# Splitting the state-space front of a hybrid kernel over two scans

## The chip, the cores and the metric

One core of a Trainium2 chip. The metric is the time of one execution in device microseconds. A core has a matrix engine (TensorE, PE in the profile; PEld is its weight load), a vector engine (VectorE, DVE), a scalar engine (ScalarE, ACT), GpSimd (POOL) and the queue that starts transfers (SyncE, SP). Each takes its instructions in the order written and waits for the others on semaphores. Matrix products land in PSUM, eight banks of 128 x 512 f32.

## The reference

Eight pictures of 128 channels x 1024 places pass through three stages, all in f32.

```python
x = x + conv_attention(group_norm(x))            # q, k, v of width 64, softmax over 1024 places
t = tokens(x)                                    # 1024 tokens x 128 channels
t = t + mamba(layer_norm(t))                     # mamba itself returns its input + a product
t = t + moe(layer_norm(t))                       # 8 experts, top 2, 128 -> 128 -> 128
# mamba(x): xn = rmsnorm(x); z, xBC, dt = split(xn @ W_in.T)
#   xBC = silu(causal_conv4(xBC)); xs, B, C = split(xBC); dt = softplus(dt + dt_bias)
#   state = state * exp(-dt*exp(A_log)) + (dt*xs) (x) B;  y = state . C + Dp*xs   (scan over tokens)
#   return x + rmsnorm(y * silu(z)) @ W_out.T
```

## The kernel before, in words

The work is ordered by hand. Each engine has a block of code, and in each the eight pictures go through three loops: `attended` (attention), `scanned(..., scan)` (the state-space stage) and `scanned(..., experts)`. Inside, a picture has eight slots (128 tokens each); parts with a number such as 3.5 are issued in that half slot, and parts with -0.25 or 6.75 just before the main work of a slot. No planner changes that order.

**Attention** (slots j). Scores go to banks 0-3 (L608, L613), VectorE takes the row maximum (L1455), ScalarE the exponential (L1104), PE turns the probabilities (`turn`, L641) through banks 4-5, ScalarE and VectorE copy them to `pt` (L1110, L1460), and `pv` (L654), `fold_parts` (L664) and `out_projection` (L673) use banks 6-7 (`O`). `projections` and `values` (L630, slot 5) of the next picture use `O` too. `residual` adds the result to `X[channel, place]` in slot 2.5. In slot 3 of the last picture VectorE prepares all weights of the next stage (`prepare_mamba`), and from there the front of picture 0 begins.

**The front** (`front` on VectorE, `pe_parts`, `act_parts`) turns a picture into what its scan reads. In order: copy `X` (`fetch`), turn it into tokens (`turn_in`, L755), statistics (L1560), a power on GpSimd (`norms`, L483), normed tokens `xt` (`normed`, L1166) and the residual `res` (`shortcut`, L1177) on ScalarE, `turn_normed` (L768), high and low parts (`high`, `low`), `steps` (L777) and three groups of projections (`group`, L730) each followed by a `tap` and three convolution steps on VectorE (`conv`, L1583), `softplus`, `cumulate` (L808), `exponents`, `factors`, the `gates`, `silus` with a table load at each end, `turn_x` (L801), `gather_x`, `turn_b`, `inner_products` (L829) and `inner` (L1639). SP writes and spreads the decay rows through DRAM (`decay_rows`), and `c_rep`. All products of the front share four banks, `lo_banks` (0-1) and `hi_banks` (2-3).

**The scan** of picture b (slots c): `decay(c + 1)` in banks 4-5 (L840), its exponential (`decays`, L1251), `mixed` on VectorE (L1654), `output_rows` (L867, L872, L879) and `y_t` (L1712). Beside it runs the whole front of picture b + 1: its first part in slot -0.25, its last in slot 7.5. In slot 0 PE also does `out_product` (L900) of picture b - 1 in `hi_banks`, and VectorE adds `res` to it (`output`, L1678). GpSimd makes `xdt`, and after slot 7 `decayed` (L514) and `weighted` (L524) of the next picture. In the last scan the front's place is taken by the start of the experts.

**Experts**: 16 halves per picture, bound by PE (L730 to L732, L983) and VectorE (L1832). The change doesn't touch them.

## Time and profile before

| | us |
|---|---|
| median of 3 runs | 1183.36 |
| lowest, highest | 1164.72, 1186.14 |
| the profiled execution | 1162.93 |
| its span, first to last instruction | 1161.1 |

The span is the profiled execution's own time less 1.8 us around it. The rows of the trace are from that execution alone. PEclk is the granted clock of TensorE: 1.00 is 2.4 GHz, 0.50 is 1.2 GHz, and a value between is a mean over a stretch that holds both.

### The profile page before, as it was taken

The numbers are of one execution on the slowest core, as the hardware profiler recorded it, in microseconds if no ns is written. First come the engines' busy times: TensorE is split into PE (matmuls) and PEld (weight loads), VectorE is DVE, ScalarE is ACT, GpSimd is POOL, SyncE is SP. The second block draws the span as 40 slices with busy tenths as digits, with TensorE's granted clock in tenths as the row PEclk, the third lists the DMA queues.
The fourth block names the chain that finished last, engine by engine and source line by source line (L and its number), as shares of the span: only waits on it lengthen the run. The fifth ranks groups of instructions, "written<-read, shape, count | busy, mean of one in ns | idle before, by whom it ended". The sixth has DMA issues, their size and how long they took to land.

```text
span 1161.1 us, 19636 instructions
## 1 busy us (share of the span) xinstructions
PE 939.0 (81%) x7630; PEld 730.8 (63%) x7630; DVE 708.1 (61%) x1846; ACT 547.2 (47%) x867; POOL 200.6 (17%) x186
## 2 busy tenths in 40 slices
PE   4689889988855678788687778698678999999998
PEld 2545565555533557576565656576567888888887
DVE  2865655565625365636556464646566888788875
ACT  1434444444433545454544535454532556555553
POOL 0000000000010505133150605142160111110100
PEclk9898899888975779888887979888888999999999
DMA  4300000000000203030301103030310000000000
GB/s 144 108 1 19 19 19 1 19 19 19 1 1 13 51 3 61 1 64 1 63 1 39 26 5 59 1 64 2 63 57 1 1 19 19 20 19 19 13 8 38
DMA packets 29613, 31.88 MB, mean 27 GB/s; under 512 B 4561, under 2 KB 24657, under 8 KB 29521
## 3 DMA queue, kind: packets, MB, share of 16 engines
q1 hardware_dynamic: 29520, 30.62, 10.8%
q8 instruction: 62, 1.02, 0.4%
q14 instruction: 31, 0.25, 0.1%
HBM read 17.24 MB, written 4.98 MB: 19 GB/s over the span
## 4 chain that ended last, share of the span: by engine, by line
PE 56%; DVE 26%; ACT 10%; issue 4%; POOL 3%; DMA 1%; SPq 1%; DVEq 0%; ACTq 0%; POOLq 0%
PE ps L983 6%; PE ps L654 5%; DVE cacc L1583 5%; PE ps L641 4%; DVE acc L1832 3%; PE ps L900 3%; POOL rs L483 3%; PE ps L630 3%; PE ps L879 2%; PE ps L872 2%; PE ps L840 2%; PE ps L867 2%; PE ps L730 2%; PE ps L888 2%; PE ps L731 2%
## 5 line engine op out<-in xcount | busy, mean ns | idle before, releaser
L1832 DVE SCALAR_TENSOR_TENSOR acc<-ps,comb,acc 128x128 f32<-128x128 f32 x512 | 141.2, 343 | 21.6 <-PE ps L983 20.9
L983 PEld LDWEIGHTS ps<-w_f,hid 128*128 128x128 f32 x1024 | 131.2, 191 | 16.5 <-ACT hid L1320 8.2
L983 PE MATMUL ps<-w_f,hid 128*128 128x128 f32 x1024 | 136.8, 277 | 4.8 <-ACT hid L1320 4.8
L1320 ACT ACTIVATE hid<-ps,b_f 128x512 f32<-128x512 f32 x128 | 86.2, 685 | 107.9 <-PE ps L732 107.6
L1251 ACT ACTIVATE dcy<-ps 128x1024 f32<-128x1024 f32 x64 | 65.7, 1027 | 141.8 <-PE ps L840 141.7
L1654 DVE SCALAR_TENSOR_TENSOR dcy<-dcy,g_sb 128x1024 f32<-128x1024 f32 x64 | 86.4, 1351 | 61.5 <-ACT dcy L1251 61.3
L1455 DVE TENSOR_REDUCE nmax<-ps 128x1 f32<-128x1024 f32 x64 | 78.1, 1220 | 40.0 <-PE ps L613 39.6
L1583 DVE SCALAR_TENSOR_TENSOR cacc<-ps,cw,cacc 128x1023 f32<-128x1023 f32 (+5 forms) x72 | 92.0, 1278 | 12.5 <-ACT cacc L1190 10.7
L1110 ACT ACTIVATE pt<-ps 128x512 f32<-128x512 f32 x64 | 38.1, 596 | 117.5 <-PE ps L641 117.2
L1460 DVE COPY pt<-ps 128x512 f32<-128x512 f32 x64 | 44.0, 688 | 76.7 <-PE ps L641 76.5
L641 PEld LDWEIGHTS ps<-id_f,probs 128*128 128x128 f32 x512 | 65.8, 156 | 34.6 <-issue 22.0
L1712 DVE TENSOR_TENSOR y_t<-ps,zs 128x256 f32<-128x256 f32 x64 | 26.7, 418 | 99.6 <-PE ps L879 99.6
L1104 ACT ACTIVATE probs<-ps,nmax 128x1024 f32<-128x1024 f32 x64 | 71.2, 1113 | 30.9 <-DVE nmax L1455 28.4
L641 PE MATMUL ps<-id_f,probs 128*128 128x128 f32 x512 | 77.3, 299 | 8.0 <-DVE pt L1460 7.9
L496 POOL TENSOR_TENSOR xdt<-xs,dts 128x256 f32<-128x256 f32 x64 | 42.5, 669 | 237.4 <-PE ps L879 237.4
L483 POOL TENSOR_TENSOR rs<-bve,neg_half 128x16 f32<-128x16 f32 x8 | 29.6, 3700 | 256.6 <-DVE bve L1569 256.6
L654 PE MATMUL ps<-pt,v_f 128*64 128x512 f32 x256 | 65.4, 617 | 3.2 <-DVE xl L1574 2.0
L867 PE MATMUL ps<-cacc,d_diag 128*128 128x128 f32 x256 | 52.7, 338 | 18.4 <-issue 16.0
L730 PE MATMUL ps<-uh,w_h 128*128 128x512 f32 x128 | 61.1, 477 | 0.0
L867 PEld LDWEIGHTS ps<-cacc,d_diag 128*128 128x128 f32 x256 | 42.2, 231 | 22.5 <-issue 18.8
L840 PE MATMUL ps<-rhs_c,lhs_c 128*128 128x512 f32 x128 | 55.8, 524 | 0.0
L608 PE MATMUL ps<-k_a,q_a 128*128 128x512 f32 x128 | 50.7, 480 | 5.7 <-ACT probs L1104 4.0
(214 smaller groups left out, 1935.2 us busy)
## 6 DMA issues: line engine op xcount, KB each, us to landing
c_dec<-exp_dram SPq DMA_DIRECT2D x32, 256.0 KB, 5.3
X<-in_x SPq DMA_DIRECT2D x8, 512.0 KB, 3.7
q_b<-q_a SPq DMA_DIRECT2D x16, 256.0 KB, 2.9
c_rep<-cacc SPq DMA_DIRECT2D x32, 128.0 KB, 2.6
out<-o_ch SPq DMA_DIRECT2D x8, 512.0 KB, 2.6
w_f<-in_w SPq DMA_DIRECT2D x2, 512.0 KB, 3.7
cst_f<-in_sel_rows SPq DMA_DIRECT2D x1, 512.0 KB, 4.0
cst_f<-in_head_rows SPq DMA_DIRECT2D x1, 512.0 KB, 5.6
```

Source lines behind the costliest of these rows:

```text
L641: last = nc.tensor.transpose(T[:, h, k * P:(k + 1) * P], probs[:, j % 2, (4 * h + k) * P:(4 * h + k + 1) * P], id_f[:])
L654: last = nc.tensor.matmul(O[e * DV:(e + 1) * DV, h, :], v_f[u][:, k, :], pt[u][:, k, h * BANK:(h + 1) * BANK], start=(quarter == 0), stop= ...
L730: nc.tensor.matmul(o, lhs[0], rhs[0], start=True, stop=False)
L840: done = nc.tensor.matmul(ps[:, 4 + h, :], lhs_c[u][:, c, :], rhs_c[u][:, 4 * h:4 * h + 4, :].rearrange("p h t -> p (h t)"), start=True, s ...
L867: nc.tensor.matmul(o[:, g, :], d_diag[:, g, :], cacc[u][:, g, t], start=(g == 0), stop=False, skip_group_check=True)
L983: last = nc.tensor.matmul(ps[:, Y_BANKS[n], t * P:(t + 1) * P], hid[n % 2][:, t * P:(t + 1) * P], w2_f[:, e, :], start=True, stop=True)
L1104: nc.scalar.activation(probs[:, j % 2, :].rearrange("p (a n) -> p a n", a=2), S[j % 2], ACT.Exp, bias=nmax[:, j:j + 1], accum_out=rsum[u][ ...
L1320: nc.scalar.activation(hid[n % 2][:], ps[:, 4 + n % 2, :], ACT.Gelu, bias=b1_f[:, n // 2:n // 2 + 1]).then_inc(e_hidden_ready, 1)
L1455: nc.vector.tensor_reduce(nmax[:, j:j + 1], S[j % 2], AX_XY, ALU.max, negate=True).then_inc(max_ready, 1)
L1583: ins = nc.vector.scalar_tensor_tensor(cacc[u][0:rows, g, k:N], banks[:, 0:N - k], cw[0:rows, g, DCONV - 1 - k:DCONV - k], cacc[u][0:rows, ...
L1654: nc.vector.scalar_tensor_tensor(mix[c % 2][:], dcy[c % 2][:], 1.0, g_sb[u][:, c:c + 1, :].to_broadcast([P, NH, P]), ALU.min, ALU.mult).th ...
L1832: done = nc.vector.scalar_tensor_tensor(acc[u][:, tt, :], ps[:, bank, t * P:(t + 1) * P], comb[u][:, tt, e:e + 1], acc[u][:, tt, :], ALU.m ...
```

## The change

- **Pictures and tokens apart.** `xc[:, b]` now holds the pictures as loaded for attention. `X` holds tokens (`X[token, chunk, channel]`), loaded from a second host-side arrangement `x_tok` by eight transfers that ScalarE's queue issues in picture 0 (two after slot 2, six after slot 6). GpSimd adds the output bias to `X` (`x_biased`). `out_projection` gives tokens: 16 products of 64 x 64 x 128 at positions (0, 0) and (64, 64) in place of 2 of 64 x 128 x 512. `residual` is one addition. `fetch`, `turn_in` and `res` are gone; `shortcut` rewrites `X` in place.
- **Statistics in attention.** `token_statistics` and `token_moments` of picture b - 1 are in VectorE's slots 5.5 and 7 of picture b, the power in GpSimd's `attend`. Those of pictures 6 and 7 follow after attention and in scan 0.
- **Attention order.** `values` from slot 5 to 5.5, `v_parts` from 5.5 to 6, `early_pv` from 6, 6.5, 7, 7.5 to 6.5, 7, 7, 7.5. One `pt` in place of two, with one more wait in slot 4.
- **Weight preparation** is cut into nine parts over pictures 2 to 6 (slots 0.5 and 6.5).
- **The front in two parts.** In scan b the late part (`cumulate` to `inner`) of picture b + 1 has slots -0.25 to 4, and the early part (`turn_normed` to the convolutions) of picture b + 2 slots 4 to 7.5. In scan 0 all are one slot later. `cacc` and `dts` have three buffers. `out_product(b - 1)` now waits for the last convolution of picture b + 1 (for the last two pictures: of the last `inner`). `gates` 1 wait for `output` of picture b - 1. GpSimd's `decayed` and `weighted` are in slots 3.5 and 4.5.
- **Between attention and scan 0**: the front of picture 0 begins in picture 7 of attention (`turn_normed` slot 3, group 0 slot 5, its convolution slots 5 to 7); the late part of picture 0 and the early part of picture 1 are written out by hand, partly among the last `pv`, `fold_parts` and `out_projection`; five convolution steps and one more of picture 1 stand in scan 0 (`second_front`).

The diff, cut to its core:

```diff
+        xc = asb("xc", [P, B, N])
+        cacc = [msb("cacc0", [P, 3, N]), cacc_1, cacc_2]
+        def slot_of(b, at):
+            return min(at + (b == 0), NT - 0.5)
...
# GpSimd
+            for b in range(B):
+                if b == 0:
+                    pool.wait_ge(tokens_loaded[0], 16 * 2)
+                elif b == 2:
+                    pool.wait_ge(tokens_loaded[1], 16 * (B - 2))
+                xb = X[:, b, :].rearrange("p (t c) -> p t c", c=P)
+                nc.gpsimd.tensor_tensor(xb, xb, b_o[:]...to_broadcast([P, NT, P]), ALU.add).then_inc(x_biased, 1)
+            decayed_at, weighted_at, norms_at = 3.5, 4.5, 2.5
...
# TensorE
-                for e in range(2):
-                    r = slice(64 * e, 64 * e + 64)
-                    last = nc.tensor.matmul(O[:, 1 - e, :], w_o[r, :], o_n[r].rearrange("p j v -> p (j v)"), ...)
+                for j in range(NT):
+                    for e in range(2):
+                        r = slice(64 * e, 64 * e + 64)
+                        last = nc.tensor.matmul(O[r, j // 4, j % 4 * P:(j % 4 + 1) * P], o_n[r, j, :], w_o[r, :],
+                                                start=True, stop=True, tile_position=(64 * e, 64 * e))
-            projections_at, values_at = 3, 5
-            early_pv = [6, 6.5, 7, 7.5]
+            projections_at, values_at = 3, 5.5
+            early_pv = [6.5, 7, 7, 7.5]
...
             def out_product(b):
                 pe.wait_ge(m_gated_ready, NT * b + NT)
-                if not isinstance(b, int) or b < B - 1:
-                    pe.wait_ge(m_inner_ready, b + 2)
+                if b + 2 < B:
+                    pe.wait_ge(m_conv_ready, 3 * (b + 2) + 3)
+                else:
+                    pe.wait_ge(m_inner_ready, B)
...
-            pe_parts = [(turn_normed, (), 1.5), (group, (0, 0), 3), (group, (0, 1), 3), (steps, (), 3),
-                        (group, (1, 0), 3.5), (group, (1, 1), 3.5), (group, (2, 0), 4.5),
-                        (group, (2, 1), 4.5), (cumulate, (), 5), (gates, (0, 0), 6), (gates, (0, 1), 6),
-                        (gates, (1, 0), 6), (gates, (1, 1), 6), (turn_x, (0,), 6), (turn_x, (1,), 6),
-                        (turn_b, (), 6.75), (inner_products, (), 7.5)]
+            pe_parts = [(cumulate, (), 1, -0.25), (gates, (0, 0), 1, 0.5), (gates, (0, 1), 1, 0.5),
+                        (gates, (1, 0), 1, 1.5), (gates, (1, 1), 1, 1.5), (turn_x, (0,), 1, 2.5),
+                        (turn_x, (1,), 1, 2.5), (turn_b, (), 1, 3), (inner_products, (), 1, 3.5),
+                        (turn_normed, (), 2, 4), (steps, (), 2, 5), (group, (0, 0), 2, 5), (group, (0, 1), 2, 5),
+                        (group, (1, 0), 2, 5.5), (group, (1, 1), 2, 5.5), (group, (2, 0), 2, 6.75),
+                        (group, (2, 1), 2, 6.75)]
...
# ScalarE
+                    if first and j in (2, 6):
+                        for k in range(2) if j == 2 else range(2, B):
+                            nc.scalar.dma_start(X[:, k, :], x_tok[k]).then_inc(tokens_loaded[j // 4], 16)
-            act_parts = [(fetch, (), 0), (normed, (), 1.5), (high, (), 2), (shortcut, (), 2.5),
-                         (steps, (), 3), (tap, (0,), 3), (softplus, (), 4.75), (tap, (1,), 4.75),
-                         (factors, (), 5), (tap, (2,), 5), (silus, (), 6), (gather_x, (), 7),
-                         (gather_b, (), 7.5)]
+            act_parts = [(factors, (), 1, 0), (shortcut, (), 1, 0.5), (silus, (), 1, 1.5), (gather_x, (), 1, 2.75),
+                         (gather_b, (), 1, 3.5), (normed, (), 2, 3.5), (high, (), 2, 4.5), (steps, (), 2, 5.5),
+                         (tap, (0,), 2, 5.5), (softplus, (), 2, 6), (tap, (1,), 2, 6), (tap, (2,), 2, 7)]
...
# VectorE
+            preparations = {(2, 6.5): (scale_weights, ()), (3, 0.5): (scale_outputs, ()), (3, 6.5): (high_weights, ()),
+                            (4, 0.5): (decay_operands, (0, 0)), (4, 6.5): (decay_operands, (0, 1)),
+                            (5, 0.5): (decay_operands, (1, 0)), (5, 6.5): (decay_operands, (1, 1)),
+                            (6, 0.5): (low_weights, ()), (6, 6.5): (small_weights, ())}
-                return [(statistics, (), -0.25), (low, (), 2), (conv, (0, 1), 3.5), (conv, (0, 2), 3.5),
-                        (conv, (0, 3), 3.5), (steps, (), 3.5), (conv, (1, 1), 4), (conv, (1, 2), 4),
-                        (conv, (1, 3), 4), (softplus, (0,), 4.5), (softplus, (1,), 4.5),
-                        (exponents, (), 4.5), (conv, (2, 1), 5), (conv, (2, 2), 5), (conv, (2, 3), 5),
-                        (ends, (), 7), (inner, (), 7.5)]
+            dve_parts = [("exponents", (), 1, -0.25), ("ends", (), 1, 1), ("inner", (), 1, 4), ("low", (), 2, 4.5),
+                         ("steps", (), 2, 5.5), ("conv", (0, 1), 2, 5.5), ("conv", (0, 2), 2, 5.75),
+                         ("conv", (0, 3), 2, 6), ("softplus", (0,), 2, 6), ("softplus", (1,), 2, 6),
+                         ("conv", (1, 1), 2, 6.5), ("conv", (1, 2), 2, 6.75), ("conv", (1, 3), 2, 7),
+                         ("conv", (2, 1), 2, 7.5), ("conv", (2, 2), 2, 7.5), ("conv", (2, 3), 2, 7.5)]
+            statistics_at, moments_at = 5.5, 7
```

## Rows read from the trace of the kernel before

**Rows 1.** The page: the chain that ended last, share of the span by engine.

```profile
PE 56%; DVE 26%; ACT 10%; issue 4%; POOL 3%; DMA 1%; SPq 1%; DVEq 0%; ACTq 0%; POOLq 0%
```

**Rows 2.** Windows: stretch, us; busy PE, PEld, DVE, ACT, POOL; PEclk, DMA share, GB/s.

```profile
159.10:196.80 37.70, 33.98 (x169) 21.71 (x169) 21.34 (x26) 17.05 (x28) 0.00 (x0) 0.91 0.07 15
...
309.00:334.20 25.20, 11.32 (x61) 9.22 (x62) 15.78 (x45) 12.64 (x29) 3.28 (x3) 0.70 0.00 0
334.20:391.80 57.60, 37.66 (x162) 25.17 (x161) 20.13 (x32) 21.33 (x25) 6.98 (x6) 0.68 0.16 32
...
585.70:650.70 65.00, 50.85 (x574) 40.96 (x574) 36.87 (x74) 32.44 (x52) 19.44 (x18) 0.84 0.14 29
...
846.00:893.30 47.30, 37.27 (x500) 30.94 (x499) 30.45 (x94) 14.06 (x25) 16.20 (x15) 0.78 0.10 35
```

**Rows 3.** Windows of short stretches in an attention picture and in scan 3.

```profile
203.30:206.70 3.40, 1.23 (x5) 0.71 (x5) 3.31 (x4) 2.97 (x5) 0.00 (x0) 0.96 0.64 139
206.70:213.40 6.70, 6.70 (x28) 6.14 (x28) 2.46 (x3) 1.80 (x3) 0.00 (x0) 0.51 0.04 8
...
618.30:622.90 4.60, 0.00 (x0) 0.00 (x0) 4.49 (x6) 0.98 (x1) 0.00 (x0) 0.99 0.00 0
623.00:632.90 9.90, 8.38 (x52) 6.35 (x53) 7.36 (x17) 3.22 (x6) 0.62 (x1) 0.50 0.08 23
```

**Rows 4.** Timeline of PE, attention picture 4: start, us, instruction [idle before].

```profile
206.67 3.67 PE L630 MATMUL ps<-w_v,xn 128*128 128x64 f32 x16 [2.06 <-DVE k_a L1440]
...
232.60 1.13 PE L673 MATMUL ps<-o_n,w_o 64*128 64x512 f32 x4
```

**Rows 5.** Timeline of PE, last picture of attention, from slot 5 on.

```profile
320.03 2.30 PE L641 MATMUL ps<-id_f,probs 128*128 128x128 f32 x8 [4.96 <-DVE pt L1460]
...
332.27 1.94 PE L768 MATMUL ps<-id_f,xt 128*128 128x128 f32 x8 [6.54 <-ACT res L1177]
```

**Rows 6.** Timeline of DVE, the end of the first front.

```profile
389.55 1.22 DVE L1639 TENSOR_TENSOR g_sb<-ps,tri_f 128x1024 f32<-128x1024 f32 x1 [14.16 <-PE ps L829]
391.83 1.58 DVE L1654 SCALAR_TENSOR_TENSOR dcy<-dcy,g_sb 128x1024 f32<-128x1024 f32 x1 [1.06 <-ACT dcy L1251]
```

**Rows 7.** Timeline of DVE: the first `mixed` of scans 3, 4 and 7.

```profile
583.43 2.80 DVE L1654 SCALAR_TENSOR_TENSOR dcy<-dcy,g_sb 128x1024 f32<-128x1024 f32 x1 [0.57 <-ACT dcy L1251]
...
648.38 1.58 DVE L1654 SCALAR_TENSOR_TENSOR dcy<-dcy,g_sb 128x1024 f32<-128x1024 f32 x1 [0.57 <-ACT dcy L1251]
...
843.32 1.60 DVE L1654 SCALAR_TENSOR_TENSOR dcy<-dcy,g_sb 128x1024 f32<-128x1024 f32 x1 [0.57 <-ACT dcy L1251]
```

**Rows 8.** Timeline of PE in scan 3.

```profile
624.52 0.69 PE L808 MATMUL ps<-dec_a,tri_f 128*128 128x64 f32 x2 [6.30 <-DVE dec_a L1613]
...
647.96 3.81 PE L900 MATMUL ps<-w_out,y_t 128*128 128x128 f32 x32
```

**Rows 9.** Timeline of ACT in scan 3: the two table loads around `silus`.

```profile
632.52 1.28 ACT L1203 ACT_TABLE_LOAD   x1
...
638.94 1.28 ACT L1209 ACT_TABLE_LOAD   x1
```

**Rows 10.** Timeline of SP, picture 0: one transfer's issue.

```profile
43.54 0.47 SPq L400 DMA_DIRECT2D q_b<-q_a  x1
```

**Rows 11.** Groups: line, engine, operation, tiles, shapes xcount | busy us, mean ns | idle before.

```profile
L1583 DVE SCALAR_TENSOR_TENSOR cacc<-ps,cw,cacc 128x1023 f32<-128x1023 f32 (+5 forms) x72 | 92.0, 1278 | 12.5 <-ACT cacc L1190 10.7
L1654 DVE SCALAR_TENSOR_TENSOR dcy<-dcy,g_sb 128x1024 f32<-128x1024 f32 x64 | 86.4, 1351 | 61.5 <-ACT dcy L1251 61.3
...
L1251 ACT ACTIVATE dcy<-ps 128x1024 f32<-128x1024 f32 x64 | 65.7, 1027 | 141.8 <-PE ps L840 141.7
...
L1166 ACT ACTIVATE xt<-ps,rnb,rs 128x128 f32<-128x128 f32 x64 | 23.2, 467 | 22.1 <-POOL rnb L487 22.1
...
L1712 DVE TENSOR_TENSOR y_t<-ps,zs 128x256 f32<-128x256 f32 x64 | 26.7, 418 | 99.6 <-PE ps L879 99.6
...
L524 POOL TENSOR_TENSOR xw<-xs,wend 128x1024 f32<-128x1024 f32 (+1 forms) x16 | 33.7, 2122 | 0.0
```

504 lines of the change are left out of this document (301 added, 203 removed).

## The prediction

> **What bounds the kernel now.** Read the page's chain first. TensorE holds 56% of it and VectorE 26%, with ScalarE, GpSimd and transfers in between [rows 1]: no single engine sets the time, a chain through all of them does. Then cut the span into its stages. An attention picture takes 37.7 us with PE busy for 34.0, so it is nearly full. From 309 to 391.8 us comes the passage to the scans, 82.8 us at clocks of 0.70 and 0.68 with PE busy for 11.3 + 37.7. A scan takes 65.0 us, in which PE is busy for 50.9 at a mean clock of 0.84, VectorE for 36.9 and ScalarE for 32.4 [rows 2]. The first `mixed` of scan 0 is at 391.8 and that of scan 7 at 843.3 [rows 6, 7], so the mean period is (843.3 - 391.8) / 7 = 64.5 us, and 317.8 us follow (scan 7 and the experts).
>
> PE's own work in a scan, at the full clock, is about 50.9 x 0.84 = 43 us. The other 22 us are waits and the low clock. The waits are the front's: PE stands for 6.30 us before `cumulate`, for VectorE's convolutions and softplus [rows 8]; it is idle from 618.3 to 622.9, and after it the clock is 0.50 for 9.9 us [rows 3], which costs some 4 to 5 us more. All of the front of picture b + 1 must pass within scan b, for it begins in its slot 0 and `inner` ends it after slot 7. That is the bound the change is aimed at.
>
> **Part 1, attention, seven pictures up to 309 us.** PE waits 2.06 us for `k_low` before `values`, and `values` with what follows runs 6.7 us at a clock of 0.51 [rows 3, 4]. One turn of probabilities (about 1.0 us; the 2.30 of one at the low clock halves to 1.15 [rows 5]) now goes first. It fills about half of the wait: -1.0 us. PE was busy for 1.23 of the 3.4 us before the clock fell [rows 3] and will be for some 2.2. If the clock then stays up, half of 6.7 us, 3.4, is saved; if not, nothing. I take the middle, -1.7. `out_projection` grows from 4 instructions in 1.13 us [rows 4] to 32 narrower ones. One of 128 columns costs 3.81 / 32 = 0.12 us when alone [rows 8]; by that it is 3.8 us, and 1.9 if the two positions run beside each other. The 64-row pair of before, two products of 512 columns in 1.13 us where eight passes at that price (4 blocks of 128 columns x 4) are 1.9, shows that pairs do overlap: +0.8, bound +2.7. It stands between `divide` and `residual`, which `projections` wait for, so it counts. VectorE gets the statistics, 2.7 us, and a seventh of the weight preparation, 1 us; its 21.3 busy of 37.7 [rows 2] leave room, so 0, bound +3.7 if each delays a maximum. Sum -1.9 per picture, -13 for seven; between -4.4 and +5.4 each. Eight transfers issued by ScalarE at 0.47 us [rows 10] are 3.8 us of its queue in picture 0, the exponentials of that picture and the next behind them: +2. GpSimd's eight additions run while it has nothing else. The second copy of `x` adds 4 MB before about 80 us; the first `q_b` of picture 2 may wait a little (0 taken, bound +4). The changed wait on the single `pt` is for a product that PE has already passed: 0. Attention: -11.
>
> **Part 2, the passage, 82.8 us.** In the last picture two stops go: 4.96 us, where PE waits behind the weight preparation on VectorE, and 6.54, where it waits for statistics, power, `normed` and `shortcut` [rows 5]. In exchange the last picture carries `normed` twice (8 x 0.47 each [rows 11]), `high`, one group and three convolutions (1.28 each [rows 11]). Slots run at some 2.6 us there, so the last turn ends about 309 + 13 + 5 = 327 instead of 336. After it (clock times of the trace of before): the last `pv` with group 1 and 2, `fold_parts` until 343; `exponents` 347, since they stand on VectorE behind two convolutions of group 2 that follow `divide`; gates 350; the block of `silus` from first to last table load is 7.7 us [rows 9], silus done at 355; `c_rep` through SP 5 us, 360; `inner_products` and `inner` (which ended at 390.8 [rows 6]) 363. VectorE then does the early part of picture 1 before it starts scan 0: `low` 1.2, `steps`, tap, three convolutions 3.8, softplus 2, in all 12 us, 375; `shortcut` and `decays(0)` on ScalarE end at about 376. Of that PE does some 33 us at the full clock, and this stretch ran at 0.68 [rows 2]; most of PE's low-clock work lies beside the others, +4. First `mixed` 380 against 391.8: -12. Bounds -22 (all products beside VectorE) and 0 (each at the low clock).
>
> **Part 3, scans 1 to 5.** Walk the cycle, with t = 0 where VectorE ends the last convolution of group 2 (now in slot 7.5, behind `y_t` of slot 7). `out_product` waits for it (3.8 us [rows 8]); then `cumulate`, `decay(1)`, `output_rows(0)`, increments, gates 0, `decay(2)`: 10.7. Its exponential 1.0, `mixed` 1.2, `output` 2.2: 15.2. Gates 1 wait for that `output`; they and the rest of the 7.7 us block of `silus` end at 22. `decays(3)` stands behind the block on ScalarE, so `mixed(3)` and `y_t` are late there. ScalarE then has `decays`, `gather_x`, `gather_b` and `normed` (3.8 by the rows' mean, overlapped 2.9) in a row [rows 11]; `high` ends at 32.5 and `low` at 35.1. `steps`, group 0 and `output_rows(5)` on PE: 41. From there VectorE never stops: nine convolutions 11.5, `mixed(7)` 1.2, two `y_t` 0.8 [rows 11], steps, softplus and one more `y_t` 3.4: 58. So the cycle is closed again, only turned round: the early part's end on VectorE now holds up `out_product`, as `inner` did. What has gone from it is the statistics, the power and `normed` ahead of `turn_normed`, `turn_in`, and part of the 6.3 us wait. What is late next is VectorE's run of 17 us at the end, with PE idle for about 7 of the last 12 us. A stretch like it (618.3 to 622.9) was followed by a clock of 0.50 [rows 3]; half of the first 6 us, 3, and 1.5 behind the waits for `output` and the narrow `steps` give 62.5, and GpSimd's moved work 0.5: 63 us, against 64.5. Bounds: 42 (PE's 43 less `turn_in`, nothing waiting) and 77 (42 at a clock of 0.68, 62, and 15 of waits). I take 63, near the walk. Five scans: 315.
>
> **Part 4, scans 0, 6 and 7.** Scan 0 has no `out_product`, but five to six more convolutions (7 us) and all parts one slot later: 62. Scan 6 has only a late part: `inner` at about 33, then slots 5 to 7 at 3 us, no run of convolutions: 44. This is the surest gain, 20 us. Scan 7 and the experts are as before, 317.8.
>
> One rule of the Trainium skill speaks against the change. GpSimd's `weighted` (2.1 us an instruction [rows 11]) stood beside one `mixed` per scan, the first: that took 2.80, 1.58 and 1.60 us [rows 7] where the mean of all is 1.35 [rows 11]. The page "SBUF — State Buffer", section "SBUF: two separate sides", says that a VectorE instruction with two SBUF inputs and a GpSimd instruction exclude each other for the whole instruction. By that rule the trace agrees (`mixed` reads two SBUF tiles), and `decayed` and `weighted`, now in slots 3.5 and 4.5, meet `mixed(5)` and `mixed(6)`.
>
> **Sum.** 391.8 - 11 - 12 = 368.8; + 62 + 315 + 44 + 317.8 = 1107.6; + 1.8 around the span = 1109.4, against 1162.93 of the profiled execution. The median of the three runs shown is 1183.36, 20 above it, and the lowest is 1164.72. I put 6 of those 20 on top: 1115.
>
> **Rivals.**
> - *The split works in full.* The chain no longer closes on itself, and a scan takes what its engines need with little waiting, 52 us (PE 42 and 10 of waits). Six scans less 10 each: 1055. For it: no engine is busy for more than 51 of 65 us. Against: the walk, where `out_product` waits for the convolutions. 0.13.
> - *The chain is only turned round, and the clock gives nothing.* Attention as before, scans 0 to 5 at 65: 391.8 - 12 + 390 + 44 + 317.8 + 1.8 = 1133. For: all parts still share four banks in one order. 0.23.
> - *GpSimd blocks the middle of the scan.* `mixed(5)` and `mixed(6)` lie on the path to `low`; each loses up to 1.6 us (2.80 less 1.2 [rows 7]), less the 0.5 taken and 0.4 no longer lost at the start. Two us more in six scans: 1121 to 1127. 0.17.
> - *Slower: the low clock fills the scan.* If VectorE's run of 17 us leaves PE at 1.2 GHz for as large a share as in the passage (0.68 [rows 2]), a scan takes 77 us: 6 x 14 = 84 more, 1199. It decides above 72 us a scan. Against: three quarters of the scan keep PE as dense as before. 0.05.
>
> **Chances.** The forecast 0.42, the rivals 0.13, 0.23, 0.17 and 0.05. The range 1062 to 1158 takes in the first three and half of what lies between the last and the forecast. Two per cent, about what a measurement of this kernel tells from no change, is 23 us: faster 0.85 (the second rival lies near the edge), within 0.10, slower 0.05.
>
> **What would show it.** Right: scan period of scans 1 to 5 at 61 to 65, scan 6 near 44, first `mixed` near 369; PE's longest wait before `out_product`, released by a convolution (`cacc`), and none before `cumulate`; VectorE without gaps from `y_t` of slot 5 to slot 7.5; no wait of `turn_normed` for `xt`; the clock up where `values` run in attention. Wrong: a period under 56 or above 67, attention pictures above 38 us, the clock near 0.7 in scans, or a wait for `x_updated` or `tokens_loaded` in attention.

## Result, and the profile after

| | median, us | lowest to highest | runs |
|---|---|---|---|
| kernel before | 1174.04 | 1162.19 to 1186.14 | 4 |
| changed kernel | 1118.02 | 1115.9 to 1120.57 | 4 |

The ratio is 0.959, with a 95% interval of 0.953 to 0.965: faster. Two runs of the kernel before (1183.36 and 1186.14 us) fell into a slower state that some executions show whatever the kernel; the ratio leaves them out, and against the other two (1162.19 and 1164.72) the gain is 45 us, where the two medians of the table are 56 apart. The forecast was 1115. The profiled execution took 1116.23 us (span 1114.4), where the sum of the prediction was 1109.4; that execution is the one to compare term by term. The kernel before is the noisier of the two (24 us between its extremes, against 4.7 here), so the stages below are compared in the two profiled executions: 1162.93 and 1116.23, 46.7 us apart.

The page of the changed kernel, its busy times and its chain, where [rows 1] had PE 56%, DVE 26% and ACT 10%:

```profile
PE 928.4 (83%) x7790; PEld 737.3 (66%) x7790; DVE 712.2 (64%) x1838; ACT 542.2 (49%) x859; POOL 236.8 (21%) x194
...
PE 53%; DVE 28%; ACT 8%; issue 6%; POOL 2%; DMA 1%; SPq 1%; DVEq 0%; ACTq 0%; POOLq 0%
...
L1773 DVE SCALAR_TENSOR_TENSOR dcy<-dcy,g_sb 128x1024 f32<-128x1024 f32 x64 | 95.4, 1491 | 117.9 <-ACT dcy L1310 117.5
```

The kind of bound has not changed: still a chain through all engines. It has only become shorter. Its stages, by the starts of the residual and of the first `mixed` of each scan on VectorE (us):

| stage | before | predicted | after | after, less predicted |
|---|---|---|---|---|
| residual of picture 6 | 309.04 | 298.0 | 293.51 | -4.5 |
| passage, to the first `mixed` | 82.8 | 70.8 | 71.8 | +1.0 |
| scan 0 | 62.4 | 62 | 63.6 | +1.6 |
| scans 1 to 5 together | 324.0 | 315 | 318.6 | +3.6 |
| scan 6 | 65.2 | 44 | 47.7 | +3.7 |
| from scan 7 to the end of the span | 317.8 | 317.8 | 319.2 | +1.4 |

The last column adds up to 6.8 us, which is the difference between 1116.2 and 1109.4. The windows of the changed kernel that answer to [rows 2]: one attention picture, the passage, scan 0, scan 3 and scan 6 (columns as in [rows 2]).

```profile
153.46:188.46 35.00, 31.58 (x197) 20.42 (x197) 24.60 (x46) 16.98 (x28) 3.28 (x3) 1.00 0.07 16
293.50:365.30 71.80, 50.16 (x276) 37.87 (x276) 36.99 (x74) 37.63 (x59) 12.76 (x11) 0.83 0.13 26
365.30:428.90 63.60, 48.95 (x532) 39.04 (x532) 42.00 (x69) 31.64 (x51) 18.42 (x16) 0.77 0.14 30
554.60:619.20 64.60, 51.39 (x566) 42.79 (x565) 35.20 (x54) 31.65 (x51) 19.07 (x15) 0.82 0.14 29
748.62:796.31 47.69, 43.16 (x533) 35.95 (x532) 20.24 (x33) 23.80 (x36) 20.30 (x15) 0.81 0.20 40
```

The passage went from clocks of 0.70 and 0.68 to 0.83. Scan 3 has the busy times and nearly the clock of before (50.9 busy at 0.84 then): the split front made the full scans barely shorter, by 5.4 us in all five. The gain lies in three other places: attention (15.5 us), the passage (11.0), and scan 6, which no longer carries an early part (17.5). Scan 0 and the last stage take back 1.3 and 1.4. Attention and a part of the passage are tested by runs below. That scan 6 is shorter for want of an early part is read from its rows; no run isolates it.

**Attention.** TensorE around `values` of picture 4 after the change, to be laid beside [rows 4]:

```profile
198.21 2.00 PE L660 MATMUL ps<-w_v,xn 128*128 128x64 f32 x16 [0.34 <-DVE k_a L1524]
...
203.56 1.08 PE L684 MATMUL ps<-pt,v_f 128*64 128x512 f32 x4 [1.51 <-DVE v_f L1533]
...
221.43 1.96 PE L705 MATMUL ps<-w_o,o_n 64*64 64x128 f32 x32
```

The wait before `values` fell from 2.06 to 0.34, and the same 16 products take 2.00 us instead of 3.67: the clock stays at 1.00, the upper of its two levels. `out_projection` is at the predicted 1.9. A wait that I had not named, 1.51 us for `v_f`, is new, and so is one of 0.66 for `pt`; the wait for `X` before the projections fell from 1.02 to 0.29. PE is therefore idle almost as long as before, 3.4 us of a picture instead of 3.7 (35.00 less 31.58, 37.70 less 33.98 [rows 2]). What became shorter is the time of the products, by 2.4 us, or 3.2 without the 0.8 that `out_projection` adds.

**Scan 3.** VectorE and TensorE from one turn to the next; t = 0 of the prediction's walk is 553.4 here.

```profile
553.69 6.19 PE L947 MATMUL ps<-w_out,y_t 128*128 128x128 f32 x32 [2.83 <-DVE cacc L1682]
...
570.04 0.80 PE L763 MATMUL ps<-xh,w_zh 128*128 128x512 f32 x1 [2.94 <-DVE X L1798]
...
592.87 0.38 PE L810 MATMUL ps<-w_dt,xh 128*128 128x16 f32 x1 [3.04 <-DVE xl L1673]
...
607.89 0.50 PE L763 MATMUL ps<-xh,w_xh 128*128 128x512 f32 x1 [2.25 <-DVE cacc L1682]
```

```profile
567.83 2.15 DVE L1798 SCALAR_TENSOR_TENSOR X<-ps,srs,X 128x128 f32<-128x128 f32 x8
...
579.24 1.22 DVE L1773 SCALAR_TENSOR_TENSOR dcy<-dcy,g_sb 128x1024 f32<-128x1024 f32 x1 [8.78 <-ACT dcy L1310]
...
582.30 2.31 DVE L1773 SCALAR_TENSOR_TENSOR dcy<-dcy,g_sb 128x1024 f32<-128x1024 f32 x1 [1.50 <-ACT dcy L1310]
...
587.32 2.77 DVE L1773 SCALAR_TENSOR_TENSOR dcy<-dcy,g_sb 128x1024 f32<-128x1024 f32 x1 [2.37 <-ACT dcy L1310]
...
591.60 1.22 DVE L1673 TENSOR_TENSOR xl<-ps,xh 128x1024 fp32r<-128x1024 f32 x1
...
601.61 0.42 DVE L1836 TENSOR_TENSOR y_t<-ps,zs 128x256 f32<-128x256 f32 x1 [7.66 <-PE ps L924]
...
618.09 1.21 DVE L1773 SCALAR_TENSOR_TENSOR dcy<-dcy,g_sb 128x1024 f32<-128x1024 f32 x1
```

GpSimd beside the two slow `mixed`:

```profile
581.44 5.12 POOL L536 TENSOR_TENSOR c_dec<-c_dec,c_rep 128x896 f32<-128x896 f32 x2 [2.25 <-DMA c_rep<-cacc]
...
587.10 4.33 POOL L546 TENSOR_TENSOR xw<-xs,wend 128x1024 f32<-128x1024 f32 x2
```

`cumulate` waits for nothing any more, and `out_product` waits 2.83 us for the last convolution. It then takes 6.19 us, where [rows 8] had 3.81: it runs at the lower clock level. PE has two more waits of the same size, 2.94 us for `output` and 3.04 for `low`. From `y_t` of slot 5 at 601.61 on, VectorE has no gap until the next turn at 619.3.

### The profile page after: what moved, and what is told of

It reads as the page before. It is cut to its first block, busy times and chain, and to the rows that moved or that the text cites. A ratio compares the mean times of both kernels' runs of the same rounds, so it can differ in the third digit from the quotient of the medians.

```text
span 1114.4 us, 20011 instructions
## 1 busy us (share of the span) xinstructions
PE 928.4 (83%) x7790; PEld 737.3 (66%) x7790; DVE 712.2 (64%) x1838; ACT 542.2 (49%) x859; POOL 236.8 (21%) x194
## 3 DMA queue, kind: packets, MB, share of 16 engines
q1 hardware_dynamic: 29520, 30.68, 11.3%
## 4 chain that ended last, share of the span: by engine, by line
PE 53%; DVE 28%; ACT 8%; issue 6%; POOL 2%; DMA 1%; SPq 1%; DVEq 0%; ACTq 0%; POOLq 0%
PE ps L1028 6%; DVE cacc L1682 6%; PE ps L684 5%; PE ps L947 4%; PE ps L763 3%; DVE acc L1959 3%; PE ps L765 3%; PE ps L764 3%; PE ps L671 3%; DVE nmax L1539 2%; PE ps L638 2%; ACT X L1234 2%; ACT un L1354 2%; PE ps L883 2%; PE ps L643 2%
## 5 line engine op out<-in xcount | busy, mean ns | idle before, releaser
L1773 DVE SCALAR_TENSOR_TENSOR dcy<-dcy,g_sb 128x1024 f32<-128x1024 f32 x64 | 95.4, 1491 | 117.9 <-ACT dcy L1310 117.5
L1028 PEld LDWEIGHTS ps<-w_f,hid 128*128 128x128 f32 x1024 | 131.2, 191 | 16.5 <-ACT hid L1373 8.2
L518 POOL TENSOR_TENSOR xdt<-xs,dts 128x256 f32<-128x256 f32 x64 | 58.3, 913 | 211.6 <-PE ps L924 211.6
L671 PEld LDWEIGHTS ps<-id_f,probs 128*128 128x128 f32 x512 | 60.0, 144 | 32.5 <-issue 22.9
L671 PE MATMUL ps<-id_f,probs 128*128 128x128 f32 x512 | 70.0, 280 | 8.7 <-ACT pt L1169 6.7
L684 PE MATMUL ps<-pt,v_f 128*64 128x512 f32 x256 | 63.6, 611 | 9.3 <-DVE v_f L1533 9.3
L947 PE MATMUL ps<-w_out,y_t 128*128 128x128 f32 x256 | 44.9, 357 | 20.4 <-DVE cacc L1682 20.4
L505 POOL TENSOR_TENSOR rs<-bve,neg_half 128x16 f32<-128x16 f32 x8 | 23.2, 2903 | 180.2 <-DVE bve L1587 180.2
L763 PE MATMUL ps<-uh,w_h 128*128 128x512 f32 x128 | 61.1, 477 | 0.0
L947 PEld LDWEIGHTS ps<-w_out,y_t 128*128 128x128 f32 x256 | 43.6, 270 | 20.7 <-issue 20.7
L883 PE MATMUL ps<-rhs_c,lhs_c 128*128 128x512 f32 x128 | 50.5, 480 | 7.0 <-ACT dcy L1310 7.0
L933 PEld LDWEIGHTS ps<-ones_f,sqt 128*128 128x128 f32 x256 | 43.4, 226 | 19.0 <-DVE y_t L1836 13.6
```

The costliest lines, as they stand in the source:

```text
L671: last = nc.tensor.transpose(T[:, h, k * P:(k + 1) * P], probs[:, j % 2, (4 * h + k) * P:(4 * h + k + 1) * P], id_f[:])
L684: last = nc.tensor.matmul(O[e * DV:(e + 1) * DV, h, :], v_f[u][:, k, :], pt[:, k, h * BANK:(h + 1) * BANK], start=(quarter == 0), stop=(qu ...
L763: nc.tensor.matmul(o, lhs[0], rhs[0], start=True, stop=False)
L883: done = nc.tensor.matmul(ps[:, 4 + h, :], lhs_c[u][:, c, :], rhs_c[u][:, 4 * h:4 * h + 4, :].rearrange("p h t -> p (h t)"), start=True, s ...
L947: last = nc.tensor.matmul(cols(hi_banks, c, P), y_t[:, g, c * P:(c + 1) * P], w_out[:, g, :], start=(g == 0), stop=(g == 1))
L1028: last = nc.tensor.matmul(ps[:, Y_BANKS[n], t * P:(t + 1) * P], hid[n % 2][:, t * P:(t + 1) * P], w2_f[:, e, :], start=True, stop=True)
```

## Experiments

Twelve kernels were run, in three groups, each on one chip and beside the kernel before on that chip. The median of the kernel before was 1166.66, 1171.87 and 1161.51 us in the three; the changed kernel, run once more in the third, gave 1118.61 against the first 1118.02. The first two groups had no run of the changed kernel on their chip. Differences "to the changed kernel" below go by these two numbers; differences under 3 us are read from the stages alone. "Scans 1 to 5" are always the five periods of the profiled execution.

### The order in attention, taken back and done alone

Taken back in the changed kernel:

```diff
-projections_at, values_at = 3, 5.5
+projections_at, values_at = 3, 5
-early_pv = [6.5, 7, 7, 7.5]
+early_pv = [6, 6.5, 7, 7.5]
-... statistics_at, moments_at = 1.5, 2.5, 5.5, 7
+... statistics_at, moments_at = 1.5, 2.5, 6, 7
-... v_at = 1.5, 4, 4.5, 6
+... v_at = 1.5, 4, 4.5, 5.5
```

> The changed kernel with the old slots in attention (values 5, v_parts 5.5, first pv 6; the statistics go to slot 6 so that they do not stand before v_parts). Theory: the 2.65 us per picture come from the order alone, by a shorter wait before values and by the clock that stays up behind it. Then a picture takes 37.5 to 38.5 us again, the clock is near 0.50 for about 6.8 us in each, and the kernel takes 18 to 24 us more, near 1140. Rival: the shorter picture comes from the single addition of the residual and the other rearrangements, and the order does nothing: within 4 us of the changed kernel.

Measured: 1138.95 us (1132.01 to 1141.37), ratio to before 0.977 (0.969 to 0.984), 21 us above the changed kernel. The last four pictures take 37.7 to 37.8 us again (the six periods are 38.3, 36.2, 37.8, 37.8, 37.7 and 37.7) and the residual of picture 6 starts at 310.72. In this run the row and the clock of before are back, here `values` and the window behind them:

```profile
207.27 3.68 PE L660 MATMUL ps<-w_v,xn 128*128 128x64 f32 x16 [2.08 <-DVE k_a L1524]
```

```profile
207.20:213.90 6.70, 6.63 (x28) 6.18 (x28) 2.45 (x4) 1.47 (x2) 0.00 (x0) 0.50 0.05 10
```

In the picture that takes 36.2 us `values` waited just as long, but ran at the upper level, and the clock fell only behind them (0.95 over that picture, 0.91 over those of 37.8):

```profile
133.32 2.00 PE L660 MATMUL ps<-w_v,xn 128*128 128x64 f32 x16 [2.08 <-DVE k_a L1524]
```

In the pictures of 37.8 us PE is idle for 3.0 us (37.80 less 34.82), less than the 3.4 of the changed kernel's 35.0. So the whole gain of the order lies in the clock and none in the sum of the waits.

Done alone, in the kernel before:

```diff
-projections_at, values_at = 3, 5
+projections_at, values_at = 3, 5.5
-early_pv = [6, 6.5, 7, 7.5]
+early_pv = [6.5, 7, 7, 7.5]
-... v_at = 1.5, 4, 4.5, 5.5
+... v_at = 1.5, 4, 4.5, 6
```

> The kernel before with nothing changed but the slots of values (5.5), v_parts (6) and the pv (6.5, 7, 7, 7.5). Theory (order and clock): 34 to 35 us a picture (its out_projection is 0.8 us shorter than the changed kernel's), 18 to 25 us less than before in all. Rival (the rest of the change shortens the picture): within 5 us of before.

Measured: 1149.78 us (1142.83 to 1165.72), ratio 0.983 (0.976 to 0.990), 17 us under the kernel before on that chip. `values` fall to 2.00 us with a wait of 0.35:

```profile
195.81 2.00 PE L630 MATMUL ps<-w_v,xn 128*128 128x64 f32 x16 [0.35 <-DVE k_a L1440]
```

Pictures take 34.6 us, 3.1 less, and the first `mixed` comes at 373.33 instead of 391.83. So this order (a turn of probabilities ahead of `values`, `v_parts` and the first `pv` half a slot later) is worth all that attention gained and a little more; its three moves were not tried one by one. The changed kernel's pictures are 0.4 us longer (35.0); its `out_projection` costs 0.8 there. In the profiled execution 11.2 of the 18.5 us reach the end: scan 6 took 69.4 us there, against 65.2 before.

### The weight preparation put back in one place

```diff
-preparations = {(2, 6.5): (scale_weights, ()), (3, 0.5): (scale_outputs, ()), ...}
+preparations = {}
...
+                    if last and j == 3:
+                        prepare_all()
```

> The changed kernel with all nine parts of the weight preparation in slot 3 of the last picture, as before. Theory: PE waits for VectorE there as it did (4.96 us), so 4 to 6 us more, all of it before the first mixed. Rival: the earlier pictures get shorter by as much without the parts: within 1 us. A third: other waits of the last picture hide it, 0 to 2 us more.

Measured: 1123.66 us (1121.59 to 1128.7), ratio 0.964 (0.959 to 0.968): 5 to 6 us more than the changed kernel, as the first account has it. The last picture takes 43.0 us against 34.8 and the first `mixed` comes at 374.48, 9.2 later. The wait of 4.96 us for `pt` of [rows 5] is back at 4.00:

```profile
304.96 0.66 PE L671 MATMUL ps<-id_f,probs 128*128 128x128 f32 x4 [4.00 <-DVE pt L1551]
```

In the span the two profiles differ by 12.5 us, 9.2 of them here; the medians say 5 to 6.

### GpSimd's two steps put back at the end of the scan (a miss)

```diff
-                if slot == slot_of(b, decayed_at) and not last:
-                    decayed(b + 1, 1 - u)
-                if slot == slot_of(b, weighted_at) and not last:
-                    weighted(b + 1, 1 - u)
...
+                        decayed(b + 1, 1 - u)
                         operand(b + 1, 1 - u, 0)
+                        weighted(b + 1, 1 - u)
```

> The changed kernel with GpSimd's decayed and weighted behind slot 7 again. Theory: mixed(4) and mixed(5), which took 2.31 and 2.77 us in scan 3, fall to 1.22, and they lie on the way to low: 2 to 2.6 us less in each of scans 1 to 5, 8 to 15 us in all; the blocked mixed(0) at the start costs nothing, for PE waits for the convolution. Rival: they have slack, or the lost time is taken back at the start, where xdt(0) is late: within 4 us.

Measured: 1130.9 us (1128.64 to 1133.32), ratio 0.970 (0.965 to 0.975): 12 to 13 us slower than the changed kernel, where I had expected a gain. Scans 1 to 5 took 67.3, 65.2, 70.4, 65.9 and 66.8 us. The trace shows both halves. `mixed(4)` and `mixed(5)` are at 1.23 us again. But GpSimd's instructions now stand beside VectorE's unbroken run at the end of the scan, where nothing is idle:

```profile
530.55 1.23 DVE L1771 SCALAR_TENSOR_TENSOR dcy<-dcy,g_sb 128x1024 f32<-128x1024 f32 x1 [1.51 <-ACT dcy L1308]
...
550.96 2.67 DVE L1771 SCALAR_TENSOR_TENSOR dcy<-dcy,g_sb 128x1024 f32<-128x1024 f32 x1
...
554.74 1.28 DVE L1702 TENSOR_SCALAR dtw<-dte 128x64 f32<-128x64 f32 x1
```

```profile
548.41 4.13 POOL L536 TENSOR_TENSOR c_dec<-c_dec,c_rep 128x896 f32<-128x896 f32 x2
...
554.06 3.35 POOL L546 TENSOR_TENSOR xw<-xs,wend 128x1024 f32<-128x1024 f32 x2
```

```profile
554.88 0.80 PE L761 MATMUL ps<-xh,w_xh 128*128 128x512 f32 x1 [4.10 <-DVE cacc L1680]
```

Even the small softplus step at 554.74, 0.18 us in the changed kernel, takes 1.28, and PE waits 4.10 us before group 2 instead of 2.25. From `mixed(7)` to the first `mixed` of the next scan VectorE takes 12.7 us in each of the five full scans of the changed kernel, and 15.7 to 16.0 in this run: 3 us a scan, about what the scans lost. The cost that I had priced at 0.5 us a scan is real, about 2.6 us on the two `mixed`; but the place the change gave these steps is better than the old one.

### What sets the full scans: output first, filler, cumulate first

Three single edits of the changed kernel. The first lets VectorE do `output(b - 1)` before `mixed(2)`, which stands ahead of it in a wait:

```diff
+                    if c == 1 and not first:
+                        output(b - 1, 1 - u)
                     if c < NT - 1:
                         mixed(b, u, c + 1)
-                    if c == 1 and not first:
-                        output(b - 1, 1 - u)
```

> The changed kernel with output(b - 1) ahead of mixed(2) on VectorE in slot 1. Theory: gates 1 wait for it (2.94 us in scan 3, on the path to silus), and it waits for nothing that is late; about 1.7 us of idle VectorE before mixed(2) and its 1.2 us leave the path, 2 to 3 us less in each of scans 1 to 5, and more where the clock no longer falls behind that wait: 10 to 25 us less in all. Rival: mixed(2) is then late and output_rows(2) takes its place as the last wait: within 3 us.

Measured: 1104.45 us (1098.52 to 1107.89), ratio 0.944 (0.936 to 0.951), 14 us under the changed kernel. Scans 1 to 5: 59.2, 61.5, 61.4, 61.5, 61.4. The wait for `X` before the gates is gone, and `silus` passes both gates in one go:

```profile
569.35 1.94 ACT L1260 ACTIVATE zs<-ps 128x1024 f32<-128x1024 f32 x2
```

The second fills two waits of PE at the turn with products whose result nobody reads, 8 before the last `y_t` and 11 before the last convolution:

```diff
+                            if b < B - 1:
+                                pe.wait_ge(m_gated_ready, NT * b - 1)
+                                filler(6, 8)
                             pe.wait_ge(m_gated_ready, NT * b)
                             sum_of_squares(b - 1, NT - 2)
                             sum_of_squares(b - 1, NT - 1)
+                            if b < B - 1:
+                                pe.wait_ge(m_conv_ready, 3 * (b + 1) + 2)
+                                filler(1, 11)
                             out_product(b - 1)
```

> The changed kernel with products nobody reads on PE in its two waits at the end of a scan: 8 before the wait for y_t(7), 11 between the sums of squares and out_product. They only keep PE busy. Theory: out_product runs at a clock of 0.50 in scans 1 to 5 (6.2 to 6.6 us instead of 3.8) because of the waits; with them filled it takes 3.8 us and each scan is 2 to 3 us shorter, 8 to 14 in all. Rival: the low clock there has another cause or is moved elsewhere: within 4 us, or longer by the filler itself.

Measured: 1107.92 us (1105.17 to 1119.61), ratio 0.950 (0.938 to 0.962), 10 us under the changed kernel. `out_product` takes 3.74 to 3.81 us in the five full scans:

```profile
551.08 2.70 PE L941 MATMUL ps<-ones_f,id_f 128*128 128x128 f32 x22
...
554.05 3.81 PE L952 MATMUL ps<-w_out,y_t 128*128 128x128 f32 x32 [0.27 <-DVE cacc L1693]
```

PE does more work and the kernel is faster: what `out_product` lost in the changed kernel, 2.4 us in scan 3, is the clock that falls in the waits at the turn, and nothing in `out_product` itself. Scans 1 to 5 together are 308.2 us against 318.6.

Part of the gain is given back further on. Here is the stretch from `mixed(4)` to `mixed(5)` of scan 3, in which PE does `inner_products`, first in the changed kernel, then with the filler:

```profile
582.30:587.32 5.02, 5.02 (x65) 4.31 (x63) 2.65 (x3) 4.67 (x12) 5.02 (x4) 1.00 0.02 5
```

```profile
578.98:588.24 9.26, 9.26 (x63) 7.67 (x63) 2.76 (x3) 4.65 (x12) 8.16 (x5) 0.50 0.01 3
```

The low clock has gone from the turn and turned up here, in scans 2 to 4, which is what the second account had allowed for. It costs 4.2 us there; by `mixed(3)` the filler had put scan 3 3.7 us ahead. The version with `output` first has the same 9.26 us at 0.50 in scans 2 to 4.

The third puts work with a far shorter wait at the turn: `cumulate` ahead of the sums of squares, and `decay(1)` ahead of `out_product`:

```diff
+                            pieces(b, -0.25)
                             sum_of_squares(b - 1, NT - 2)
                             sum_of_squares(b - 1, NT - 1)
+                            decay(b, u, 1)
                             out_product(b - 1)
-                    pieces(b, c - 0.25)
-                    if c + 1 < NT:
-                        decay(b, u, c + 1)
+                    if c > 0 or first:
+                        pieces(b, c - 0.25)
+                        if c + 1 < NT:
+                            decay(b, u, c + 1)
```

> The changed kernel with cumulate before the sums of squares and decay(1) before out_product on PE. Both need nothing of the last convolution. Theory: the head of the cycle is out_product, then cumulate, exponents, decay(1), mixed(1); with them out of it VectorE makes exponents and mixed(1) while out_product runs, and only output_rows(0), increments and gates 0 stay behind it: 1.5 to 2.5 us less per scan, 7 to 13 in all. Rival: the cycle is closed by engines' work and not by this order: within 3 us.

Measured: 1109.41 us (1106.82 to 1117.59), ratio 0.952 (0.943 to 0.960), 9 us under. Scans 1 to 5: 66.4, 62.0, 61.0, 61.9, 61.1. `out_product` waits 1.14 us instead of 2.83 and is still 6.28 us long, so what is gained at the turn is of the chain, not of the clock. The two edits of order together:

> Both of the last but one and the first of this set together (cumulate and decay(1) ahead of out_product; output ahead of mixed(2)). Theory: two different waits of one chain, so the gains add: 17 to 35 us less than the changed kernel. Rival: after one of them another branch ends last: no more than the better of the two.

Measured: 1091.24 us (1090.25 to 1095.16), ratio 0.935 (0.929 to 0.940), 27 us under the changed kernel, where the two alone gave 14 and 9. Scans 1 to 5: 62.4, 58.7, 61.0, 57.8, 58.1. The clock at the turn is still the lower one, by the window of its `out_product`:

```profile
553.60:560.00 6.40, 6.40 (x36) 6.40 (x36) 2.92 (x7) 3.50 (x10) 2.31 (x2) 0.60 0.10 28
```

### The last convolutions shortened (a miss in size)

Is VectorE's run at the end the bound of the scan? For pictures 2 to 7 the second and third step of group 2 work on 8 columns only; the rest of these two steps is left out of the computation.

```diff
+                    end = k + 8 if b >= 2 and g == 2 and k >= 2 else N
-... cacc[b % 3][0:rows, g, k:N], banks[:, 0:N - k], ...
+... cacc[b % 3][0:rows, g, k:end], banks[:, 0:end - k], ...
```

> The changed kernel with the second and third convolution step of group 2 done for 8 columns only, for pictures 2 to 7; the rest of those two steps is left out. It takes 2 x 1.1 us from VectorE's run before out_product in scans 0 to 5. Theory: that run closes the cycle, so each of those scans is 2.2 us or more shorter (more where PE then waits less and its clock stays up): 13 to 25 us in all. Rival: another chain ends beside it (products or ScalarE), and it has slack: within 4 us.

Measured: 1113.22 us (1110.26 to 1116.11), ratio 0.959 (0.954 to 0.963). That is 5.4 us under the changed kernel run beside it, between what the two accounts expected, so it decides for neither. The wait before `out_product` fell to 0.73 us, and `out_product` to 5.44:

```profile
553.55 5.44 PE L947 MATMUL ps<-w_out,y_t 128*128 128x128 f32 x32 [0.73 <-DVE cacc L1683]
```

Scans 1 to 5 took 62.7, 61.7, 61.2, 65.1 and 61.2, in all 311.9 against 319.1 in the changed kernel beside it; and scan 6 took 52.7 against 45.3, which gives the whole of it back in this execution. Scan 6 has no convolutions, and the edit takes nothing from it; what grew is the clock's part. From its `mixed(4)` on it ran like this:

```profile
767.60:776.90 9.30, 9.30 (x63) 7.82 (x63) 2.75 (x3) 1.65 (x5) 8.19 (x5) 0.50 0.00 1
776.90:793.59 16.69, 16.69 (x173) 12.30 (x173) 6.51 (x9) 4.67 (x8) 1.85 (x3) 0.62 0.00 1
```

In the changed kernel beside it the first of these stretches took 5.00 us at 1.00, and the second this:

```profile
786.40:797.74 11.34, 10.81 (x170) 8.15 (x163) 8.06 (x8) 4.80 (x8) 6.79 (x5) 1.00 0.01 3
```

PE was busy without a gap at the lower level; what let the clock fall there, this run does not show. What it does show is that VectorE's run at the end counts, for less than its length.

### Filler in the best version, and `silus` in another order

The changed kernel stood beside these two and the one with short convolutions, unedited:

> The changed kernel, unchanged, on the chip of the next three: 1114 to 1122 us. It is the measure for them.

Measured: 1118.61 us (1115.64 to 1121.02, 6 runs), ratio 0.964 (0.961 to 0.967): the first result again.

The filler of 8 products ahead of the last `y_t`, added to the version with both edits of order:

> The kernel with cumulate, decay(1) and output ahead, and with 8 unread products on PE before its wait for y_t(7). Theory: out_product there still runs at 0.50 (6.24 us); if PE's wait of 2.15 us is what lets the clock fall, it takes 3.8 us and scans 1 to 5 are 1 to 2.5 us shorter, 5 to 12 in all, near 1082. Rival: the remaining waits of the run (1.6 and 1.1 us) are enough to let it fall: within 4 us of 1091.

Measured: 1093.05 us (1087.97 to 1105.4), ratio 0.945 (0.939 to 0.951); without its highest run the median is 1091.47: no gain. `out_product` stays wholly or partly at the lower clock in four of the five full scans (5.0 to 6.6 us). In three of them a wait of 1.3 us is left in front of it that this filler doesn't cover:

```profile
547.77 6.57 PE L952 MATMUL ps<-w_out,y_t 128*128 128x128 f32 x32 [1.32 <-DVE cacc L1693]
```

That wait alone does not decide it: in scan 4 it is as long, 1.31 us, and `out_product` takes 3.81.

Last, in that kernel the block of `silus` takes its three convolution results before the two gates, because `c_rep` (through SP's queue) and with it `inner_products` wait for the third of them:

```diff
-                for g in range(2):
-                    act.wait_ge(m_z_product, 3 * b + 2 + g)
-                    nc.scalar.activation(two(zs[u][:, g, :]), ...)
...
+                for g in range(2):
+                    act.wait_ge(m_z_product, 3 * b + 2 + g)
+                    nc.scalar.activation(two(zs[u][:, g, :]), ...)
```

> As the one before, and ScalarE's silus takes the three convolution results before the two gates. Theory: in the changed kernel the block waited 3.7 us for gates 1, but with output ahead that wait is gone, so the order inside the block of 7.4 us changes little; c_rep starts 3 us earlier, but inner_products wait for gather_x too: within 3 us of the one before. Rival: turn_x(0) and c_rep are on the path: 1 to 3 us less per scan, 6 to 18 in all.

Measured: 1077.03 us (1074.47 to 1079.27), ratio 0.928 (0.924 to 0.933): 16 us under the one before by the medians, 14 without that kernel's highest run and 12.6 in the profiled executions; 41 to 42 under the changed kernel, and the fastest of all. Scans 1 to 5: 55.7, 58.2, 58.4, 54.1, 58.2. The transfer is issued 15.5 us after the `mean_square` that marks the scan (559.86 less 544.40), against 17.4 in the kernel without this edit (566.10 less 548.68). SP's issue of it here, then VectorE's mark:

```profile
559.86 2.45 SPq L460 DMA_DIRECT2D c_rep<-cacc  x4
```

```profile
544.40 0.15 DVE L1800 TENSOR_SCALAR sve<-ps 128x8 f32<-128x8 f32 x1
```

The same two in the kernel without the edit:

```profile
566.10 2.44 SPq L460 DMA_DIRECT2D c_rep<-cacc  x4
```

```profile
548.68 0.15 DVE L1800 TENSOR_SCALAR sve<-ps 128x8 f32<-128x8 f32 x1
```

The transfer goes 1.8 to 2.0 us earlier in each of the five scans. Yet this is not what made them shorter: without the edit they took 62.4, 57.8, 58.8, 60.7 and 58.2 us, so scans 2, 3 and 5 stayed within 0.4 us, and scans 1 and 4 lost 6.7 us each, 13.3 in all. From `mixed(4)` to `mixed(6)` of scan 1, without the edit and with it:

```profile
449.93:465.78 15.85, 15.27 (x111) 11.89 (x110) 6.68 (x6) 7.00 (x15) 8.78 (x6) 0.53 0.00 1
```

```profile
451.96:461.30 9.34, 7.47 (x100) 5.76 (x100) 6.06 (x7) 7.17 (x15) 8.61 (x6) 1.00 0.01 2
```

Scan 4 shows nearly the same numbers (15.86 us at 0.53, 9.35 at 1.00), and in scan 3 the stretch takes 10.44 us at 0.87 without the edit and 10.25 at 0.87 with it. So the gain is 6.5 us of clock in the middle of each of two scans. The rival's result came, and its reason, that `c_rep` is on the path, is not borne out by the three scans in which `c_rep` came earlier and nothing followed. Why the clock stays up with this order is not shown. The wait of PE before `decay(4)` is 2.18 us without the edit in scan 1, and split into 0.80 and 1.18 with it, which may be the reason. The edit was not tried in the changed kernel alone.

## Why the prediction was right

The time (1118.0, forecast 1115), the sign and every stage to within 5 us came as predicted, in the main for the reasons given. In attention and in the passage part of the closeness is luck: errors in two terms went opposite ways. Point by point, by its steps:

- **Part 1, attention, -11: the sign and the clock right, two terms mis-sized.** Predicted were -1.0 for the wait, -1.7 for the clock, taken as the middle between 0 and 3.4, and +0.8 for `out_projection`. The wait before `values` lost 1.7 us (2.06 to 0.34) and that before the projections 0.7, but 1.5 for `v_f` and 0.7 for `pt` came in: the waits together give only -0.3. They moved and did not go. From `values` to the first `pv` it was 6.85 us (206.67 to 213.52) and is 5.35 (198.21 to 203.56), of which 1.51 are the new wait for `v_f`: the work itself lost 3.0, near the upper end. With +0.8 that is -0.3 - 3.0 + 0.8 = -2.5 of the 2.7 by which a picture is shorter (37.7 to 35.0). So 0.7 too much for the wait stood against 1.3 too little for the clock. The sum has two slips that changed nothing: the bound of -4.4 leaves out the +0.8, and the "eight passes" that make 1.9 are sixteen (4 x 4). The +2 for ScalarE's eight issues and the bound of +4 for the second copy of `x` came to nothing: the seventh residual is 15.5 us earlier, and the first of all, 83.3 against 83.6, is not late. The two runs with the order of attention show that this edit carries the whole term: 17 us when taken back, 20 when done alone (309.04 less 289.08), at the residual of picture 6.
- **Part 2, the passage, -12: right, -11.0.** The two stops went as said: in the last picture PE's longest wait is 2.10 us, and `turn_normed` waits for nothing. The stations fit too. Counted from the residual of picture 6, `c_rep` was to be there after 51 us and PE starts `inner_products` after 50.9; from the end of `inner` to the first `mixed` 17 us were taken and 15.9 came (349.4 to 365.3). That the 51 us came out is partly luck: `silus` was done after 42.4 us, where 46 were taken, and `c_rep` then took 8.2 us from issue to PE (336.11 to 344.28) in place of 5. It is in the chain with 6.27 us, of PE's wait for it 4.45. The weight preparation, when put back, is worth 9.2 us up to the first `mixed`, 5 to 6 in the median.
- **Part 3, scans 1 to 5, 63 us: right, 63.7 in the mean (62.7, 61.9, 64.6, 64.2, 65.2).** The statement that the chain is "only turned round" held: `out_product` now waits for the last convolution, 2.83 us, and `cumulate` for nothing. It is not PE's longest wait, as I had said it would be; those for `output` and `low`, 2.94 and 3.04 us, are as long. In scan 3, counted from 553.4, `output` ended at 16.6 (walk: 15.2), `low` at 39.4 (35.1), `y_t` of slot 5 came at 48.2 (41), and VectorE's run took 16.5 us (17). The 7 us by which the walk is exceeded at slot 5 stand against the 5 that I had put on top of it as one sum. The 2.4 us in `out_product` are the clock term, and the filler shows its cause. The 0.5 for GpSimd was too small: the two `mixed` lost 1.1 and 1.5 us, and they are `mixed(4)` and `mixed(5)`, where the prediction had (5) and (6). The rule of the Trainium skill cited in the prediction ("SBUF — State Buffer", section "SBUF: two separate sides") agrees with this, and also with the 2.67 us of `mixed(7)` in the run that moved GpSimd to the end of the scan. The softplus step that took 1.28 us there has one SBUF input, of which the rule as cited says nothing. What the rule does not decide is the better place; the 12 to 13 us of that run do.
- **Part 4: scan 0 at 63.6 (62), scan 6 at 47.7 (44), the rest at 319.2 (317.8).** Scan 6, the "surest gain, 20 us", gave 17.5, and is the step that was off the most for its length. I had not given it the turn's low clock: the `out_product` at its start takes 6.45 us, and the stretch behind it ran at 0.61 and 0.78. Here are that row and the two windows:

```profile
747.71 6.45 PE L947 MATMUL ps<-w_out,y_t 128*128 128x128 f32 x32 [2.83 <-DVE cacc L1682]
```

```profile
747.00:755.00 8.00, 7.29 (x39) 7.08 (x40) 1.82 (x4) 0.00 (x0) 2.22 (x2) 0.61 0.01 2
755.00:770.00 15.00, 12.06 (x202) 9.87 (x206) 7.10 (x18) 10.65 (x18) 2.85 (x2) 0.78 0.45 86
```

That is not the whole of the 3.7 us. In the second run of the changed kernel scan 6 took 45.3 us with an `out_product` as slow, 6.29; there the part from `mixed(5)` on took 11.3 us at a clock of 1.00, and 13.5 at 0.87 here.

- **The rivals.** The full split (52 us a scan) did not come. It was nearer than its place among the rivals suggests, though: changes of order alone, with nothing removed, brought the scans to 54 to 58 us. "Only turned round" held in its first half and fell in its second, that the clock gives nothing: in attention the clock gave 3 us a picture. GpSimd's blocking held in the rows, 2.6 us on the two `mixed`, but the scans are not longer by as much. The low clock does not fill the scan; it takes 2.4 us at the turn of scan 3, and then the gates (0.52 from 570.0 to 579.5) and `steps` run at it too.
- **The 6 us added for the noise of the kernel before** were not called for by any step: the changed kernel's four runs lie within 4.7 us, and the profiled one is 1.8 below their median. Without them the forecast would have been 9 us low instead of 3; that they made up for the 6.8 by which the steps fell short is luck.

Scans of one kernel differ by 3 us with the same work: the changed kernel's scans 2 and 4 took 61.9 and 64.2 us in one execution and 64.9 and 61.9 in the other. The rows show one cause. In scan 2 `mixed(5)` starts 0.18 us before GpSimd's `weighted` and takes 1.29 us; in scan 3 `weighted` starts 0.22 us before `mixed(5)`, which takes 2.77. Scan 2:

```profile
525.77 1.29 DVE L1773 SCALAR_TENSOR_TENSOR dcy<-dcy,g_sb 128x1024 f32<-128x1024 f32 x1 [1.99 <-ACT dcy L1310]
```

```profile
525.95 4.33 POOL L546 TENSOR_TENSOR xw<-xs,wend 128x1024 f32<-128x1024 f32 x2
```

PE then waits 1.56 us for `low` instead of 3.04, most of `steps` runs at the upper level (an instruction every 0.11 us instead of 0.21), and from `mixed(5)` to `mixed(7)` it is 15.0 us instead of 18.1. The scan of 61.9 us in the other execution has its `mixed(5)` at 1.25 as well. What stays open is what else moves the clock: scan 4 of the first execution had 1.41 us there and yet ran at 0.71 behind it. So a saving of 2 us in a scan can show as 0 or as 3, and can move the low clock to another place, as the runs with the filler and with the short convolutions show.
